# A cross-interaction network on one core: chunks 4 and 5 loaded instead of picked, and a new order of TensorE's front

## The chip, the core and the metric

The kernel runs on one NeuronCore of one Trainium2 chip. The core has TensorE (PE, with its weight loads as PEld), VectorE (DVE), ScalarE (ACT), GpSimd (POOL) and SyncE (SP, which here only issues transfers). The metric is device time in microseconds (us), the median of several executions. The profile is of one further execution.

## The reference

The input is x, 64 rows of 32 fields of 64 numbers (`X0`, float32). Three layers are computed, and of each only the sum over the embedding goes into the result:

```
Xi = X0
for W, b in ((W1, b1), (W2, b2), (W3, b3)):
    Wr = W.reshape(128, 32, m)                   # m = fields of Xi: 32, 128, 128
    Xi = einsum('bhd,bmd,ohm->bod', X0, Xi, Wr) + b[None, :, None]
    pools.append(Xi.sum(axis=-1))
y = concatenate(pools) @ fc_W.T + fc_b           # 64 x 1
```

## The kernel before

The kernel has 64 x 64 = 4096 columns (row, embedding), cut into eight **chunks** of 512. For each chunk the 128 partitions of four tiles hold products of two fields (`z`), split into a high and a low part in fp32r: `feat[:, c, 0]` (hi) and `feat[:, c, 1]` (lo). TensorE multiplies them by two sets of weights: W1's (`w1_hi`, `w1_lo`) give x1 (`x1_product(c)`, 13 matmuls), and weights `a_hi`, `a_lo` folded from W3, fc_W and W2 give the factor by which x1 is multiplied (`a_product(c)`, 14 matmuls). VectorE forms that product (`product(c)`), GpSimd adds the chunks up (`gather`), and a few small matmuls give y.

**How a chunk's features are made.** The left factor is loaded (`x_in`, four buffers). The right factor is made in one of two ways. For a chunk below `PICKED` (6 before), TensorE picks it out of the split input with 0/1 weights: `pick_right(c, half)` (L567), two matmuls for each half, into PSUM (`z_ps`). For chunks from `PICKED` on, SP loads 1 MB of ready-made factors into `r_in[:, c % 2]` (`load_right`, L185). VectorE multiplies (`mult`, L461, L477), ScalarE copies the high part (`hi`, L366, L360), and the low part is the difference: of half 0 on VectorE (`lo`, L479, L484), of half 1 on GpSimd (`lo`, L262, L266). Half 0 of the product lies in PSUM (`z_ps`), half 1 in SBUF (`r_in`). `split_x(c)` splits the input itself, on ScalarE (L362) and then GpSimd (L254, L259); a picked chunk needs it before its picks, a loaded one only for the linear matmul at the end of `a_product(c)` (L627).

**The fold of the second weights.** `v_part` (L631) contracts W3 with fc_W, a transpose and three small copies give `v_st`, four `a_round`s (L657) contract it with W2, ScalarE saves each (`save_a`), SP stores each with three transfers (`store_a`, L203 to L206), reads them back skewed into `f1` (L233 to L240), and ScalarE's queue reads `f2` (L432). VectorE adds them (L530, L532) and splits them (`main_lo`, L493, and `rest_lo`, L498).

**Order.** Every engine's program is written out by hand and runs in order; semaphores tie them together. What matters below:

- SP: after W1's rest (L222) come `load_x(5)`, `load_x(6)`, the twelve stores, the reads of `f1`, `load_right(6)`, `x16` again for `xsum`, `load_x(7)`, `load_right(7)`.
- ScalarE: hi(3,1), W1's rest (L421), split_x(5), hi(4,0), hi(4,1), save_x1(0), save_x1(1), four transfers of `f2`, hi(5,0), hi(5,1), save_zz(1).
- VectorE: chunks 0 to 5, W1's `rest_lo` after mult(4,1), then the fold's adds, chunk(6), product(0), product(1), chunk(7), product(2) and on.
- GpSimd: split_x and lo in turn; after lo(5) split_x(6), the four adds of `xsum` (L345), lo(6), split_x(7), lo(7), gathers. The features of chunk 7 lie where `xsum` is still being read (`features_free`, L148), so hi(7), lo(7) wait for it.
- TensorE: the front (L670 to L708), then x1_product(2), (3), (4), a_product(0), (1), x1_product(5), a_product(2), x1_product(6), a_product(3), x1_product(7), a_product(4) to (7). x1_product(c) for c of 2 or more waits for save_x1(c - 2), since there are two banks; a_product(c) waits for product(c - 2).

Of the kernel before, what the change touches and what calls it, by code (L numbers as in the profile page):

```python
# [24 lines left out]
TERM_HI, TERM_LO, TERM_HI2, TERMS = 0, 32, 64, 96  # L25


PICKED = 6
X_BUFS = 4


# [6 lines left out]
def cin_kernel(nc, x, xl, xr, w1, w2, w3, vecs, fc_b, out):  # L38
# [9 lines left out]
    with ctx:  # L48
# [67 lines left out]
        r_here = [sem(f"r_here{i}") for i in range(2)]  # L116
# [27 lines left out]
        def count(c, half):  # L144

            return HALVES * c + half + 1
# [30 lines left out]
        @block.sync  # L177
        def _(sp):
            def load_x(c):
                if c >= X_BUFS:  # L180
                    sp.wait_ge(z_done, count(c - X_BUFS, 1))
                    sp.wait_ge(xs_lo, c - X_BUFS + 1)
                sp.dma_start(x_in[:, c % X_BUFS, :], xl[:, c * N:(c + 1) * N]).then_inc(x_here[c % X_BUFS], 16)  # L183

            def load_right(c):  # L185
                if c % 2 == 0:
                    sp.wait_ge(spread_done, 3)
                else:
                    sp.wait_ge(hi_done, count(PICKED - 1, 1))
                    sp.wait_ge(lo_done[1], PICKED)  # L190
                sp.dma_start(r_in[:, c % 2, :, :], xr[c]).then_inc(r_here[c % 2], 16)

            def load_w3(i):
                part = slice(i * 2 * M, (i + 1) * 2 * M)
                sp.dma_start(w3_sb[:, :, :].rearrange("q (g i) o -> q g (i o)", g=4)[:, :, part],  # L195
                             w3.rearrange("q (g io) -> q g io", g=4)[:, :, part]).then_inc(w3_in[i], 16)

            def load_w2(t):
                part = slice(t * N, (t + 1) * N)
                sp.dma_start(w2_sb[:, :].rearrange("o (g n) -> o g n", g=2)[:, :, part],  # L200
                             w2.rearrange("o (g n) -> o g n", g=2)[:, :, part]).then_inc(w2_in[t], 16)

            def store_a(rows, g, t, left):  # L203

                sp.dma_start(bass.AP(scratch.tensor, (left + FIELDS * t) * M, [[EXT * M, rows], [1, FIELDS * M]]),
                             at_sb[64 * g:64 * g + rows, t, :]).then_inc(a_out, 16)  # L206

            load_x(0)
            sp.dma_start(w1_sb[:, :, 0:TILES, :], w1[:, :, 0:TILES, :]).then_inc(w1_in, 16)
            load_x(1)  # L210
            load_w3(0)
            load_w3(1)
            load_x(2)
            load_w3(2)
            load_w3(3)
            load_x(3)
            load_w2(0)
            load_w2(1)
            load_x(4)
            load_w2(2)  # L220
            load_w2(3)
            sp.dma_start(w1_sb[:, :, EVEN:, :], w1[:, :, EVEN:, :]).then_inc(w1_rest_in, 16)  # L222
            load_x(5)
            load_x(6)
            for t in range(ROUNDS):
                sp.wait_ge(a_saved, t + 1)
                store_a(EXT, 0, t, 0)
                store_a(EXT, 1, t, HALF)
                store_a(H, 0, t, H)
            sp.wait_ge(zeros_done, ZEROS)  # L230
            sp.wait_ge(a_out, A_OUT)
            for j in range(J):
                sp.dma_start(f1[H * j:H * j + H, 0:TILES, :], bass.AP(  # L233
                    scratch.tensor, EXT * TILES * j * M, [[(EXT + 1) * M, H], [EXT * M, TILES], [1, M]])).then_inc(f_main_in, 16)
            for e in range(2):
                for f, first in ((f1, HALF * EXT), (f2, HALF)):
                    sp.dma_start(f[e:TERMS:2, EVEN + e, :], bass.AP(
                        scratch.tensor, first * M, [[0, 3], [(EXT + 1) * M, HALF], [1, M]])).then_inc(f_rest_in, 16)
            sp.dma_start(f1[0:TERMS, LIN, :], bass.AP(
                scratch.tensor, FC2_COL * EXT * M, [[0, 3], [M, H], [1, M]])).then_inc(f_rest_in, 16)  # L240
            load_right(PICKED)
            sp.wait_ge(lo16_done, 1)
            sp.dma_start(x16[:, :, :].rearrange("p g n -> p (g n)"),
                         x.rearrange("h (c n) -> (h c) n", c=4)).then_inc(xp_in, 16)
            load_x(7)
            load_right(PICKED + 1)
            sp.dma_start(fcb_sb[:, :], fc_b).then_inc(fcb_in, 16)
            sp.wait_ge(y_done, 1)
            sp.dma_start(out, y_sb[:, :]).then_inc(out_done, 16)
            sp.wait_ge(out_done, 16)  # L250

        @block.gpsimd
        def _(pool):
# [22 lines left out]
            for i, base in enumerate((0, H, -H)):  # L276
# [43 lines left out]
            pool.wait_ge(xs_lo, 4)  # L320
            lo(1)
            pool.wait_ge(lo_done[1], 2)
            split_x(4)
            pool.wait_ge(xs_lo, 5)
            lo(2)
            pool.wait_ge(w1_rest_in, 16)
            nc.gpsimd.tensor_tensor(w1_sb[:, 0, EVEN:, :], w1_sb[:, 0, EVEN:, :], w1_sb[:, 1, EVEN:, :],
                                    ALU.add).then_inc(w_sum, 1)
            pool.wait_ge(w_sum, 2)
            split_x(5)  # L330
            pool.wait_ge(xs_lo, 6)
            lo(3)
            lo(4)
            lo(5)
            pool.wait_ge(lo_done[1], 6)
            split_x(6)
# [21 lines left out]
        def _(act):  # L358
# [50 lines left out]
            copy(v_st[:, H:H + 8], v_by_field[:, 0, :]).then_inc(v_saved, 1)  # L409
            copy(v_st[:, H + 8:H + 15], v_by_field[:, 1, 0:7]).then_inc(v_saved, 1)  # L410
            hi(2, 0)
            split_x(4)
            hi(2, 1)
            save_a(0)
            save_a(1)
# [3 lines left out]
            hi(3, 1)  # L419
            act.wait_ge(w_sum, 2)  # L420
            copy(w1_hi[:, EVEN:, :], w1_sb[:, 0, EVEN:, :]).then_inc(w_hi_done, 1)  # L421
            split_x(5)
            hi(4, 0)
            hi(4, 1)
            act.wait_ge(vec_in, 16)
# [4 lines left out]
            for j in range(J):  # L430
                k = 1 if j == 0 else 0
                act.dma_start(f2[H * j:H * j + H, k:TILES, :], bass.AP(  # L432
                    scratch.tensor, (TILES * j + k) * M, [[(EXT + 1) * M, H], [1, (TILES - k) * M]])).then_inc(f_main_in, 16)
            hi(5, 0)
            hi(5, 1)
            save_zz(1)
            act.wait_ge(v_saved, 1)
            copy(v_rep[:, :, :], v_st[:, 0:H].rearrange("o (h r) -> o h r", r=1).to_broadcast(
# [4 lines left out]
            save_x1(3)  # L443
            act.wait_ge(f_sum, 2)
            copy(a_hi[0:TERMS, TILES:, :], f1[0:TERMS, TILES:, :]).then_inc(a_hi_done, 1)
            split_x(6)
            save_x1(4)
            act.wait_ge(q_ready, 1)
            copy(q_sb[:, :], q_ps).then_inc(q_saved, 1)
            hi(6, 0)  # L450
            hi(6, 1)
            split_x(7)
# [7 lines left out]
        def _(dve):  # L460
            def mult(c, half):  # L461
                tiles = of_half(half)
                dve.wait_ge(x_here[c % X_BUFS], 16 * (c // X_BUFS + 1))
                if c < PICKED:
                    dve.wait_ge(picked, count(c, half))
                    right = field_bank(c, half)
                    if half == 1 and c >= 2:
                        dve.wait_ge(hi_done, count(c - 2, 1))
                        dve.wait_ge(lo_done[1], c - 1)
                else:  # L470
                    dve.wait_ge(r_here[c % 2], 16)
                    right = r_in[:, c % 2, tiles, :]
                    if half == 0:
                        dve.wait_ge(z_done, count(c - 1, 1))
                        dve.wait_ge(lo_done[0], c - 1)
# [38 lines left out]
            nc.vector.tensor_tensor(x16[:, 0, :], x16[:, 0, :], x16[:, 1, :], ALU.mult).then_inc(z16_done, 1)  # L514
            mult(0, 0)
            mult(0, 1)
            dve.wait_ge(w_hi_done, 1)
            main_lo(w1_sb[:, 0, :, :], w1_hi, w1_lo, w_lo_done)
            lo(0)
            chunk(1)  # L520
            chunk(2)
            chunk(3)
            mult(4, 0)
            mult(4, 1)
            dve.wait_ge(w_hi_done, 2)
            rest_lo(w1_sb[:, 0, :, :], w1_hi, w_lo_done)
            lo(4)
            chunk(5)
            dve.wait_ge(f_main_in, F_MAIN)
            nc.vector.tensor_tensor(f1[:, 0:TILES, :], f1[:, 0:TILES, :], f2[:, 0:TILES, :], ALU.add).then_inc(f_sum, 1)  # L530
            dve.wait_ge(f_rest_in, F_REST)
# [5 lines left out]
            dve.wait_ge(f_sum, 2)  # L537
            dve.wait_ge(a_hi_done, 2)
            rest_lo(f1, a_hi, a_lo_done)
            chunk(6)  # L540
            product(0)
            product(1)
# [18 lines left out]
        def _(pe):  # L561
# [19 lines left out]
                    nc.tensor.matmul(bank, weights[:, k, :], feat[:, c, part, k, :],  # L581
                                     start=(start and k == 0), stop=False)

            def x1_hi(c, half):
                if c >= 2 and half == 0:
                    pe.wait_ge(x1_saved, c - 1)
                pe.wait_ge(w_hi_done, 1)
                pe.wait_ge(hi_done, count(c, half))
                terms(x1_ps[c % 2][:, :], c, half, w1_hi, 0, start=(half == 0))
                pe.wait_ge(w_lo_done, 1)  # L590
                terms(x1_ps[c % 2][:, :], c, half, w1_lo, 0)

            def x1_lo(c, half):
                pe.wait_ge(lo_done[half], c + 1)
# [79 lines left out]
            pick_right(0, 1)  # L674
            keep_clock(6)
            spread16(0)
            pick_right(1, 0)
            x1_hi(0, 0)
            pick_right(1, 1)
            x1_lo(0, 0)  # L680
            v_part(0)
            v_part(1)
            v_part(2)
            pick_right(2, 0)
            v_part(3)
            pick_right(2, 1)
            pe.wait_ge(ident_done, 2)
            pe.wait_ge(vt_saved, 1)
            nc.tensor.transpose(v_ps, vt_sb[:, :], ident[:, :]).then_inc(v_ready, 1)
            x1_hi(0, 1)  # L690
            a_round(0)
            pick_right(3, 0)
            a_round(1)
            pick_right(3, 1)
            a_round(2)
            a_round(3)
            pick_right(4, 0)
            x1_lo(0, 1)
            pick_right(4, 1)
            x1_hi(1, 0)  # L700
            x1_lo(1, 0)
            x1_hi(1, 1)
            pick_right(5, 0)
            x1_lo(1, 1)
            x1_tail(0)
            x1_tail(1)
            pick_right(5, 1)
            spread16(1)  # L708
            x1_product(2)
            x1_product(3)  # L710
# [79 lines left out]
```

## Time and profile before

| | us |
|---|---|
| median of 3 runs | 82.0 (81.88 to 83.26) |
| the profiled execution, its own time | 82.64 |
| its span, first to last instruction | 80.8 |
| PE busy | 75.0 (93% of the span, 372 instructions) |
| DVE, ACT, POOL busy | 47.1, 34.6, 49.8 |
| transfers | 12.01 MB |

The span is what the engines' rows cover; the time of the execution is 1.8 us longer. A matmul of 512 columns shows 0.39 us in a group's mean, because matmuls overlap; how many start per microsecond is read from the timeline, where the next group begins before the last one's end.

### The profile page before, as it was taken

The numbers are of one execution on the slowest core, as the hardware profiler recorded it, in microseconds if no ns is written. First come the engines' busy times: TensorE is split into PE (matmuls) and PEld (weight loads), VectorE is DVE, ScalarE is ACT, GpSimd is POOL, SyncE is SP. The second block draws the span as 40 slices with busy tenths as digits, with TensorE's granted clock in tenths as the row PEclk, the third lists the DMA queues.
The fourth block names the chain that finished last, engine by engine and source line by source line (L and its number), as shares of the span: only waits on it lengthen the run. The fifth ranks groups of instructions, "written<-read, shape, count | busy, mean of one in ns | idle before, by whom it ended". The sixth has DMA issues, their size and how long they took to land.

```text
span 80.8 us, 1130 instructions
## 1 busy us (share of the span) xinstructions
PE 75.0 (93%) x372; PEld 51.7 (64%) x372; DVE 47.1 (58%) x44; ACT 34.6 (43%) x51; POOL 49.8 (62%) x49
## 2 busy tenths in 40 slices
PE   4999699989999999959999999999999999999970
PEld 1326255743218677648888888888888888886850
DVE  1056999996797998497499709973003003113541
ACT  1833994579779943983836500580300300000000
POOL 4989836999993699492099989629924103261400
PEclk9999999999999999999999999999999999999999
DMA  0998999999996434369992000000000000000000
GB/s 22 252 366 250 369 370 352 381 385 392 375 322 196 128 89 110 101 215 385 353 417 89 4 4 0 4 0 0 0 0 0 0 0 8 0 0 0 0 0 0
DMA packets 7529, 12.01 MB, mean 149 GB/s; under 512 B 835, under 2 KB 3971, under 8 KB 7267
## 3 DMA queue, kind: packets, MB, share of 16 engines
q1 hardware_dynamic: 6915, 11.16, 40.3%
q10 hardware_dynamic: 608, 0.77, 3.0%
q8 instruction: 3, 0.05, 0.3%
q14 instruction: 3, 0.02, 0.1%
HBM read 10.88 MB, written 1.05 MB: 148 GB/s over the span
## 4 chain that ended last, share of the span: by engine, by line
PE 61%; DMA 14%; SPq 13%; ACT 4%; ACTq 2%; issue 2%; DVE 1%; DVEq 0%
PE a_ps L581 28%; PE x_ps L581 21%; DMA w_sb<-w 14%; SPq L183 6%; SPq L195 3%; SPq L200 2%; ACT feat L360 2%; PE x_ps L601 2%; PE a_ps L628 2%; PE z_ps L575 2%; PE a_ps L627 2%; ACTq L432 2%; PE a_ps L666 1%; PE x_ps L739 1%; ACT zz L360 1%
## 5 line engine op out<-in xcount | busy, mean ns | idle before, releaser
L266 POOL TENSOR_TENSOR feat<-r_in,feat 128x1024 fp32r<-128x1024 f32 x8 | 19.2, 2404 | 4.1 <-ACT feat L360 3.6
L581 PE MATMUL x_ps<-feat,w_hi 128*128 128x512 f32 x64 | 18.8, 393 | 0.0
L504 DVE SCALAR_TENSOR_TENSOR x<-a_ps,vec,x 128x512 f32<-128x512 f32 x7 | 5.3, 751 | 19.2 <-PE a_ps L628 19.1
L581 PE MATMUL a_ps<-feat,a_hi 128*128 128x512 f32 x64 | 16.2, 395 | 0.0
L259 POOL TENSOR_TENSOR xs<-x_in,xs 32x512 fp32r<-32x512 f32 x7 | 10.8, 1548 | 8.1 <-ACT xs L360 7.8
L273 POOL TENSOR_TENSOR x<-x 128x512 f32<-128x512 f32 x6 | 7.8, 1292 | 11.5 <-DVE x L504 11.3
L581 PEld LDWEIGHTS x_ps<-feat,w_hi 128*128 128x128 f32 x64 | 11.9, 188 | 2.6
L581 PEld LDWEIGHTS a_ps<-feat,a_hi 128*128 128x128 f32 x64 | 11.9, 188 | 2.7
L360 ACT ACTIVATE feat<-z_ps 128x1024 fp32r<-128x1024 f32 x8 | 8.2, 1025 | 7.4 <-DVE z_ps L477 6.2
L484 DVE TENSOR_TENSOR feat<-z_ps,feat 128x1024 fp32r<-128x1024 f32 x8 | 9.7, 1218 | 2.1 <-ACT feat L360 2.1
L374 ACT ACTIVATE x<-x_ps,vec 128x512 f32<-128x512 f32 x8 | 5.4, 686 | 12.3 <-PE x_ps L601 12.3
L581 PE MATMUL x_ps<-feat,w_lo 128*128 128x512 f32 x32 | 9.9, 391 | 0.0
L360 ACT ACTIVATE feat<-r_in 128x1024 fp32r<-128x1024 f32 x8 | 8.4, 1051 | 1.7 <-DVE r_in L477 1.7
L575 PE MATMUL z_ps<-xs,pick 128*128 128x512 f32 x24 | 8.8, 457 | 0.3
L581 PE MATMUL a_ps<-feat,a_lo 128*128 128x512 f32 x32 | 8.6, 390 | 0.0
L477 DVE TENSOR_TENSOR z_ps<-x_in,z_ps 128x1024 f32<-128x1024 f32 x6 | 7.3, 1224 | 1.4 <-PE z_ps L575 1.3
L575 PEld LDWEIGHTS z_ps<-xs,pick 128*128 128x128 f32 x24 | 4.1, 204 | 5.9 <-issue 4.6
L477 DVE TENSOR_TENSOR r_in<-x_in,z_ps 128x1024 f32<-128x1024 f32 x6 | 7.3, 1215 | 0.4 <-PE z_ps L575 0.4
L565 PE MATMUL x_ps<-at_sb 128*128 128x512 bf16 x17 | 6.3, 543 | 1.2 <-DVE at_sb L507 1.2
L581 PEld LDWEIGHTS x_ps<-feat,w_lo 128*128 128x128 f32 x32 | 6.0, 188 | 1.4
L581 PEld LDWEIGHTS a_ps<-feat,a_lo 128*128 128x128 f32 x32 | 6.0, 188 | 1.3
L360 ACT ACTIVATE xs<-x_in 128x512 fp32r<-128x512 f32 x8 | 5.0, 626 | 2.2 <-DMA x_in<-xl 2.1
(76 smaller groups left out, 75.3 us busy)
## 6 DMA issues: line engine op xcount, KB each, us to landing
w_sb<-w SPq DMA_DIRECT2D x9, 512.0 KB, 8.8
x_in<-xl SPq DMA_DIRECT2D x8, 256.0 KB, 7.4
r_in<-xr SPq DMA_DIRECT2D x2, 1024.0 KB, 6.1
a_by_fields<-at_sb SPq DMA_DIRECT2D x8, 96.0 KB, 2.1
x<-x ACTq DMA_DIRECT2D x1, 512.0 KB, 4.6
x<-x SPq DMA_DIRECT2D x1, 512.0 KB, 6.0
w_sb<-w SPq DMA_DIRECT2D x1, 256.0 KB, 11.7
a_by_fields<-at_sb SPq DMA_DIRECT2D x4, 64.0 KB, 2.1
```

What stands on the lines that cost most here:

```text
L183: sp.dma_start(x_in[:, c % X_BUFS, :], xl[:, c * N:(c + 1) * N]).then_inc(x_here[c % X_BUFS], 16)
L259: nc.gpsimd.tensor_tensor(xs[rows, c, :], x_in[rows, c % X_BUFS, :], xs[rows, c, :].bitcast(f32), ALU.subtract).then_inc(xs_lo, 1)
L266: nc.gpsimd.tensor_tensor(feat[:, c, 1, of_half(1), :], z_of(c, 1), feat[:, c, 0, of_half(1), :].bitcast(f32), ALU.subtract).then_inc(lo_d ...
L273: nc.gpsimd.tensor_tensor(x1[:, 0, :], x1[:, 0, :], x1[:, c, :], ALU.add).then_inc(acc_done, 1)
L360: return nc.scalar.activation(dst, src, ACT.Copy)
L374: nc.scalar.activation(x1[:, c, :], x1_ps[c % 2][:, :], ACT.Identity, bias=vec[:, 0:1]).then_inc(x1_saved, 1)
L477: nc.vector.tensor_tensor(z_of(c, half), left, right, ALU.mult).then_inc(z_done, 1)
L484: nc.vector.tensor_tensor(feat[:, c, 1, of_half(0), :], z_of(c, 0), feat[:, c, 0, of_half(0), :].bitcast(f32), ALU.subtract).then_inc(lo_d ...
L504: nc.vector.scalar_tensor_tensor(out=x1[:, c, :], in0=a_ps[:, c % 2, :], scalar=vec[:, 3:4], in1=x1[:, c, :], op0=ALU.add, op1=ALU.mult).t ...
L565: nc.tensor.matmul(x1_ps[1][:, :], blank[:, 0:M], blank[:, 0:N], start=True, stop=True)
L575: last = nc.tensor.matmul(field_bank(c, half)[:, k, :], pick[:, half * PER_HALF + k, :], xs[:, c, :], start=True, stop=True)
L581: nc.tensor.matmul(bank, weights[:, k, :], feat[:, c, part, k, :], start=(start and k == 0), stop=False)
```

## The change

Chunks 4 and 5 are loaded too: `PICKED` is 4, SP issues a load of 1 MB for chunk 4 ahead of `load_x(5)`, one for chunk 5 where chunk 6's was, and those for 6 and 7 later. VectorE, ScalarE and GpSimd do chunk 5, and split_x(4) and (5), later. VectorE does lo(0) ahead of W1's low part. On TensorE the picks of chunks 4 and 5 are gone, x1's product of chunk 0 is cut in two functions and spread ahead of the picks and of `v_part`, and the rounds of the fold stand in pairs.

```diff
-PICKED = 6
+PICKED = 4
@@ sync, load_right
-                if c % 2 == 0:
+                if c == PICKED:
                     sp.wait_ge(spread_done, 3)
                 else:
-                    sp.wait_ge(hi_done, count(PICKED - 1, 1))
-                    sp.wait_ge(lo_done[1], PICKED)
+                    sp.wait_ge(hi_done, count(max(c - 2, PICKED - 1), 1))
+                    sp.wait_ge(lo_done[1], max(c - 1, PICKED))
@@ sync, program
             sp.dma_start(w1_sb[:, :, EVEN:, :], w1[:, :, EVEN:, :]).then_inc(w1_rest_in, 16)
+            load_right(4)
             load_x(5)
             load_x(6)
...
-            load_right(PICKED)
+            load_right(5)
             sp.wait_ge(lo16_done, 1)
...
             load_x(7)
-            load_right(PICKED + 1)
+            load_right(6)
+            load_right(7)
@@ gpsimd
-            split_x(4)
-            pool.wait_ge(xs_lo, 5)
             lo(2)
             (W1's rest is added)
+            lo(3)
+            lo(4)
+            pool.wait_ge(lo_done[1], 5)
+            split_x(4)
             split_x(5)
             pool.wait_ge(xs_lo, 6)
-            lo(3)
-            lo(4)
             lo(5)
@@ scalar
             hi(2, 0)
-            split_x(4)
             hi(2, 1)
...
             copy(w1_hi[:, EVEN:, :], w1_sb[:, 0, EVEN:, :]).then_inc(w_hi_done, 1)
-            split_x(5)
             hi(4, 0)
             hi(4, 1)
...
-            hi(5, 0)
-            hi(5, 1)
             save_zz(1)
...
-            split_x(6)
             save_x1(4)
             act.wait_ge(q_ready, 1)
             copy(q_sb[:, :], q_ps).then_inc(q_saved, 1)
+            split_x(4)
+            hi(5, 0)
+            hi(5, 1)
+            split_x(5)
+            split_x(6)
             hi(6, 0)
@@ vector
+            lo(0)
             dve.wait_ge(w_hi_done, 1)
             main_lo(w1_sb[:, 0, :, :], w1_hi, w1_lo, w_lo_done)
-            lo(0)
             chunk(1)
             chunk(2)
             chunk(3)
-            mult(4, 0)
-            mult(4, 1)
             dve.wait_ge(w_hi_done, 2)
             rest_lo(w1_sb[:, 0, :, :], w1_hi, w_lo_done)
-            lo(4)
-            chunk(5)
+            chunk(4)
             dve.wait_ge(f_main_in, F_MAIN)
...
             rest_lo(f1, a_hi, a_lo_done)
+            chunk(5)
             chunk(6)
@@ tensor: x1_hi is cut into x1_main (w1_hi) and x1_low_weights (w1_lo)
+            x1_main(0, 0)
             pick_right(1, 0)
-            x1_hi(0, 0)
             pick_right(1, 1)
+            x1_main(0, 1)
             x1_lo(0, 0)
+            x1_low_weights(0, 0)
+            x1_low_weights(0, 1)
             v_part(0)
             v_part(1)
             v_part(2)
             pick_right(2, 0)
+            pick_right(2, 1)
             v_part(3)
-            pick_right(2, 1)
             (transpose of vt)
-            x1_hi(0, 1)
+            x1_lo(0, 1)
+            pick_right(3, 0)
             a_round(0)
-            pick_right(3, 0)
             a_round(1)
+            x1_hi(1, 0)
             pick_right(3, 1)
             a_round(2)
             a_round(3)
-            pick_right(4, 0)
-            x1_lo(0, 1)
-            pick_right(4, 1)
-            x1_hi(1, 0)
             x1_lo(1, 0)
             x1_hi(1, 1)
-            pick_right(5, 0)
             x1_lo(1, 1)
             x1_tail(0)
             x1_tail(1)
-            pick_right(5, 1)
             spread16(1)
```

`mult`'s wait for `r_here` counts the loads of its buffer.

## Rows read from the trace of the kernel before

**Rows 1.** The chain that ended last: start, duration, and what ran.
```profile
11.53 11.71 DMA w_sb<-w
23.29 1.08 PE a_ps L666 x4
...
34.29 0.91 ACT zz L360
...
38.73 2.74 PE x_ps L581 x12
...
48.38 2.77 PE x_ps L581 x12
```

**Rows 2.** Timeline of TensorE: start, duration, operation, count, idle time before.
```profile
24.30 0.74 PE L575 MATMUL z_ps<-xs,pick 128*128 128x512 f32 x2
...
31.39 0.62 PE L581 MATMUL x_ps<-feat,w_hi 128*128 128x512 f32 x2
...
35.24 0.50 PE L601 MATMUL x_ps<-zz,w_hi 96*128 96x512 f32 x1 [0.97 <-ACT zz L360]
```

**Rows 3.** Timeline of ScalarE between 24 and 32 us.
```profile
24.41 0.60 ACT L360 ACTIVATE at_sb<-a_ps 128x512 f32<-128x512 f32 x1 [0.56 <-PE a_ps L666]
24.91 1.05 ACT L360 ACTIVATE feat<-r_in 128x1024 fp32r<-128x1024 f32 x1
25.86 0.41 ACT L360 ACTIVATE w_hi<-w_sb 128x256 fp32r<-128x256 f32 x1
...
29.82 0.69 ACT L374 ACTIVATE x<-x_ps,vec 128x512 f32<-128x512 f32 x1 [1.18 <-PE x_ps L601]
```

**Rows 4.** Timeline of VectorE, the same columns.
```profile
27.52 0.99 DVE L498 TENSOR_TENSOR w_hi<-w_sb,w_hi 32x256 fp32r<-32x256 f32 x1
...
39.97 0.55 DVE L498 TENSOR_TENSOR a_hi<-f,a_hi 32x384 fp32r<-32x384 f32 x1 [1.15 <-ACT a_hi L360]
40.55 1.23 DVE L477 TENSOR_TENSOR z_ps<-x_in,r_in 128x1024 f32<-128x1024 f32 x1
41.81 2.19 DVE L477 TENSOR_TENSOR r_in<-x_in,r_in 128x1024 f32<-128x1024 f32 x1
43.92 1.21 DVE L484 TENSOR_TENSOR feat<-z_ps,feat 128x1024 fp32r<-128x1024 f32 x1
45.26 0.75 DVE L504 SCALAR_TENSOR_TENSOR x<-a_ps,vec,x 128x512 f32<-128x512 f32 x1
```

**Rows 5.** Timeline of GpSimd, the same columns.
```profile
26.95 1.28 POOL L259 TENSOR_TENSOR xs<-x_in,xs 32x512 fp32r<-32x512 f32 x1 [2.06 <-ACT xs L360]
...
34.43 2.38 POOL L266 TENSOR_TENSOR feat<-r_in,feat 128x1024 fp32r<-128x1024 f32 x1 [1.28 <-ACT feat L360]
40.55 2.36 POOL L259 TENSOR_TENSOR xs<-x_in,xs 32x512 fp32r<-32x512 f32 x1 [3.75 <-ACT xs L360]
43.05 3.48 POOL L345 TENSOR_TENSOR x<-x 128x512 f32<-128x512 f32 x3
...
47.13 2.40 POOL L266 TENSOR_TENSOR feat<-r_in,feat 128x1024 fp32r<-128x1024 f32 x1 [0.21 <-issue]
```

**Rows 6.** SP's queue: issue of transfers, start, duration and count.
```profile
21.15 5.54 SPq L205 DMA_DIRECT2D a_by_fields<-at_sb  x12
28.06 1.74 SPq L233 DMA_DIRECT2D f<-a_by_fields  x4
...
33.72 0.45 SPq L191 DMA_DIRECT2D r_in<-xr  x1
```

**Rows 7.** Transfers of r_in, then of W1's rest: from issue to landing.
```profile
DMA to landing us min/median/max: 5.0/6.1/7.1
...
DMA to landing us min/median/max: 11.7/11.7/11.7
```

**Rows 8.** Stretches: width, busy us of PE, PEld, DVE, ACT, POOL, granted clock, DMA share, GB/s.
```profile
18.00:20.00 2.00, 2.00 (x9) 0.78 (x8) 1.26 (x2) 2.00 (x6) 1.99 (x1) 1.00 1.05 386
24.00:26.00 2.00, 2.00 (x9) 1.42 (x8) 1.50 (x2) 1.59 (x3) 0.89 (x2) 1.00 0.72 208
```

More of the change, by code:

```diff
@@ L470, in mult @@
                 else:
-                    dve.wait_ge(r_here[c % 2], 16)
+                    dve.wait_ge(r_here[c % 2], 16 * ((c - PICKED) // 2 + 1))
                     right = r_in[:, c % 2, tiles, :]
@@ L582, in terms, with x1_main @@
                                      start=(start and k == 0), stop=False)
-            def x1_hi(c, half):
+            def x1_main(c, half):
                 if c >= 2 and half == 0:
@@ L589, in x1_hi, with x1_low_weights @@
                 terms(x1_ps[c % 2][:, :], c, half, w1_hi, 0, start=(half == 0))
+            def x1_low_weights(c, half):
+                pe.wait_ge(hi_done, count(c, half))
                 pe.wait_ge(w_lo_done, 1)
                 terms(x1_ps[c % 2][:, :], c, half, w1_lo, 0)
+            def x1_hi(c, half):
+                x1_main(c, half)
+                x1_low_weights(c, half)
             def x1_lo(c, half):
```

## The prediction

> **What bounds the kernel now.** I read the chain of waits first. From 23.29 us on it is TensorE almost alone: x1 and a products at 13 or 14 matmuls each, 12 matmuls in 2.74 to 2.77 us, so 0.23 us a matmul [rows 1]. The one hole is 0.97 us ahead of x1's tail of chunk 2, which waits for ScalarE's copy of zz, and that copy ends at 35.2 behind hi(5,0) and hi(5,1) [rows 1, 2]. Ahead of 23.29 the chain is W2's last quarter, 11.71 us from issue to landing [rows 1], on a queue that moves 386 GB/s with its engines full [rows 8]. So an edit gains in two ways only: by fewer matmuls or holes behind 23.29, and it loses wherever TensorE must wait for features. The timelines of ScalarE, VectorE and GpSimd say how near those waits are.
>
> **TensorE's own work.** The change removes the picks of chunks 4 and 5: four halves of two matmuls, 8 x 0.23 = 1.8 us. Behind the last round of the fold (starts 23.29, ends 24.4 [rows 1]; chunk 4's load is issued after W2 and W1's rest, so this stays) TensorE now has only x1_lo(1,0), x1_hi(1,1), x1_lo(1,1), 8 matmuls, to 26.2. Before, it had work without a hole from 24.30 to 31.39 and beyond [rows 2]. The reordered front ahead of 23.29 gains nothing that lasts, since the landing of W2 ends it: its moved matmuls lie there beside VectorE's multiplies. It costs nothing either, by the same cover. Pick_right(3,1) comes some 0.5 us later, mult(3,1) ends near 23.8, and hi(3,1) was held by save_a(3) until 24.91 anyway [rows 3].
>
> **The low part of W1's rest.** The tails of chunks 0 and 1 need it. ScalarE's order gives hi(3,1) at 24.91 to 25.96 and W1's rest at 25.86 to 26.27, as before [rows 3]. GpSimd's lo(3) needs only hi(3,1), so it starts at 26.0 and runs 2.40 us, as another lo does [rows 5], to 28.4. VectorE asks for rest_lo (L498) at 26.3. Rows 4 and 5 show what happens then: this line took 0.99 us from 27.52 while GpSimd's subtraction ran from 26.95 to 28.23, 0.55 us at 39.97 with GpSimd idle. It ended 0.28 us after GpSimd's ended. So rest_lo ends at 28.4 + 0.3 = 28.7. Before, this work was hidden behind picks; now TensorE waits from 26.2 to 28.7. The bound below is 26.9 (no block).
>
> **Chunk 4.** Its load of 1 MB lands behind W1's rest, which was issued at 12.3 and landed 11.7 us later, at 24.0 [rows 7]. At 386 GB/s [rows 8] 1.05 MB is 2.7 us: 26.7, so it is not what chunk 4 waits for. VectorE's in-order queue is. mult(4,0) runs 28.7 to 29.9 and mult(4,1) to 31.0 (1.23 us [rows 4], 1.1 for the second), with GpSimd idle. hi(4,1) ends at 32.1, and save_x1(0), queued behind it on ScalarE, takes 0.69 us [rows 3] to 32.8. x1_product(2) waits for that save. Before it began at 31.39 [rows 2]; between the tails with spread16(1) (to 30.1) and 32.8 TensorE waits another 2.7 us. The product's 12 matmuls end at 35.55. ScalarE's zz no longer waits behind hi(5): it issues f2 near 31.1 to 33.3 and has zz at 34.4, so the hole of 0.97 us is gone. The tail starts at 35.5 against 35.24 before. Sum up to here: **+0.25 us**. The 1.8 us of picks and the 0.97 us hole are all spent on the two new waits. x1_product(4) ends at 41.95 for 41.7 [rows 1].
>
> **The transfers behind.** Twelve stores of the fold, issued from 21.15, flowed at once; the last landed by 28.0, when the reads of f1 start [rows 6]. Now 2.7 us of load stands ahead of them in the same queue. The stores have slack in rate (208 GB/s at share 0.72 [rows 8]), so I put the last landing 1.4 us later, between 0.8 and 2.7. The loads issued from 33.72 [rows 6] shift with it: chunk 5's lands at 38.8 + 1.4 = 40.2 (5.0 us from issue [rows 7]), chunk 6's where chunk 7's was, near 44.0 + 1.4 = 45.4, bounds 44.8 and 46.7. The f1 and f2 sums have room: a_hi is needed only at 41.95, nearly 10 us after f2's transfers are issued.
>
> **Chunks 5 to 7.** Here GpSimd gets a chain that it did not have. ScalarE's queue after save_x1(4) (ends 42.7) is: q, split_x(4) to 43.3, hi(5,0), hi(5,1) to 45.15, split_x(5) to 45.7. Only then GpSimd does split_x(5), lo(5), split_x(6), xsum, lo(6). Before, lo(5) was over at 36.8 [rows 5] and this chain began at 40.55 with split_x(6). Alone these take 1.28 + 2.40 + 1.28 + 2.9 + 2.40 us with 0.5 between: 56.5 for lo(6). And VectorE's multiplies of loaded chunks block them. Rows 4 and 5: mult(6,0) and split_x(6) started together at 40.55; the multiply took 1.23, the split 2.36 instead of 1.28 us. mult(6,1) from 41.81 took 2.19 and ended 1.1 us after the split, and the adds, started at 43.05, took 3.48. So each such multiply puts 1.1 us into GpSimd's chain, and waits out the operation in flight.
>
> The Trainium skill (SBUF — State Buffer, "Who interferes with whom") speaks against the change in the same way: a VectorE instruction with two SBUF inputs contends with a GpSimd instruction that reads SBUF, whole instruction against whole instruction, and one with a PSUM input does not. By it moving two chunks' right factors from PSUM to SBUF makes four more such multiplies; the rows above agree at 1.1 us each. Were it a shared bandwidth instead, the sum would be about 1 us less.
>
> With chunk 6's load at 45.4: mult(6,0) 45.45 to 46.6, split_x(5) to 47.9, mult(6,1) to 49.0, lo(5) to 51.4. x1_product(5) starts at 48.6 (6.7 us after 41.95 [rows 1]) and wants lo(5) after 10 matmuls, at 50.9: wait 0.5. lo(6): 51.4 + 1.3 + 3.0 + 2.6 = 58.3; x1_product(6) starts 6.2 us after 49.1, at 55.3, and wants it at 57.6: wait 0.75. Then mult(7,0) to 59.5, split_x(7) to 60.8, mult(7,1) to 61.9, hi(7,1) to 63.0, lo(7) to 65.4; x1_product(7) wants it at 64.55: wait 0.9. Together 2.15 us. With the load at 46.7, mult(6,0) loses its turn to split_x(5): mult(6,1) ends at 51.65, lo(6) of VectorE and product(0), queued behind it, at 53.6, and a_product(2) waits 2.0 us for product(0) (before, product(0) was over at 46.0 [rows 4]); one more wait of 0.4. Both orders give about the same.
>
> **Sum.** 0.25 + 2.2 to 2.5 = 2.5 us. Span 80.8 to 83.3; the profiled execution was 82.64, 0.6 us above the median of 82.0, so against the median 84.5.
>
> **Rivals.**
> (1) The chain after 41.95 is milder: no block by multiplies, loads on time. Then lo(6) is ready at 56.5 and wanted at 57.3, nothing waits, and 0.25 us or, with rest_lo unblocked too, -1.4 us remain: 80.6 to 83.6, no change that can be told. For it: TensorE's slack at chunk 5 is 1.2 us. Against: 2.36 and 2.19 us in rows 4 and 5.
> (2) Faster. The features keep ahead all along: TensorE gives back 1.8 us of picks and 0.97 us of hole: 82.0 - 2.8 = 79.2. It decides if W1's low rest is ready by 26.2 and save_x1(0) by 27.6. For it: chunk 4's load is there by 26.7. Against: W1's high rest ends at 26.27 [rows 3] and four operations follow in series.
> (3) Slower yet. Chunk 6's load lands behind 47.1, in lo(5)'s time, and mult(6,0) waits until 49.5, product(0) until 55: a_product(2) waits 3.5 us: 82.0 + 4 = 86. Or TensorE's two waits of 2.6 us, 1.4 us of work between them, cost it the granted clock, which rows 8 show at 1.00 (2.4 GHz) throughout; then x1_product(2) and (3) at 1.2 GHz cost up to 3 us. The one hole shown, 0.97 us [rows 2], did not cost it, so this is bounded from one side only.
>
> **Chances.** My forecast 0.60 (83.7 to 85.3); rival 1 0.19; rival 2 0.06; rival 3 0.15 (85.3 to 87.5). I leave out rival 2 and the lower part of rival 1: range 82.6 to 86.6. About 2% can be told from no change here: faster 0.07, within 0.18 (rival 1, nearly whole), slower 0.75.
>
> **What the new profile would show.** W1's rest_lo (L498, first instance) at over 2 us beside a GpSimd lo of 2.4; TensorE idle near 26 to 28.7 at x1's tail and to 32.8 at x1_product(2), released by ScalarE's save; the tail of chunk 2 within 0.5 us of 35.24; stores landing over 0.8 us later; GpSimd busy without a hole from 45.7 to 58; TensorE waiting 0.5 to 2 us in or before a_product(2), again in x1_product(6). I am wrong if those multiplies do not lengthen GpSimd's operations, or if stores and loads are as early as before.

## The result and the profile after

| | median us | against the kernel before |
|---|---|---|
| the kernel before | 81.94 (81.85 to 83.26) | |
| the changed kernel | 87.93 (87.78 to 88.45) | 1.073, 95% interval 1.068 to 1.078 |

A ratio leaves disturbed executions out, so it can differ a little from the quotient of two medians.

The change makes the kernel 7.3% slower: 6.0 us, where 2.5 were forecast and 86.6 us was the upper end. The profiled execution's span grew from 80.8 to 86.2 us, by 5.4. That is less than 6.0 because the profiled execution of the kernel before took 82.64 us, 0.7 us above its median here, and that of the changed kernel 88.05 us, 0.1 us above. The direction and the first two waits were right; the size was not.

The page of the changed kernel, the slices of the granted clock:

```profile
PEclk9999999999999965579999999999999999999999
```

The line before showed nines throughout; here four slices between 30 and 39 us are low. Its stretches by hand (width, busy us of PE, PEld, DVE, ACT, POOL, granted clock, DMA share, GB/s):

```profile
26.80:29.30 2.50, 0.10 (x1) 0.00 (x0) 2.47 (x2) 0.00 (x0) 2.14 (x1) 1.00 0.60 203
29.30:31.00 1.70, 1.63 (x6) 0.96 (x6) 1.67 (x2) 0.42 (x1) 0.00 (x0) 0.92 0.07 22
31.00:33.40 2.40, 0.17 (x1) 0.00 (x0) 1.96 (x2) 2.23 (x4) 0.42 (x1) 0.50 0.42 117
33.40:38.40 5.00, 4.94 (x13) 3.93 (x14) 0.69 (x1) 1.80 (x4) 1.94 (x1) 0.59 0.51 153
38.40:44.50 6.10, 6.10 (x29) 5.01 (x29) 2.78 (x4) 2.31 (x4) 0.00 (x0) 1.00 0.98 377
```

TensorE stands still twice, for 2.5 and 2.4 us, with 1.6 us of work between. Its clock falls from 2.4 to 1.2 GHz: first in the stretch behind the first hole (0.92), and it is down all through the second. Windows of 0.5 us put the fall near 30.7 us and the return near 37.5 us. x1_product(2), 13 matmuls, takes from 33.4 to 38.4 us; at full clock it takes 3 (the next one, 38.44 to 41.40).

Timeline of TensorE, the changed kernel (start, duration, operation, count, idle time before and its releaser):

```profile
29.37 0.71 PE L610 MATMUL x_ps<-zz,w_hi 96*128 96x512 f32 x2 [2.46 <-DVE w_hi L501]
...
33.46 1.22 PE L582 MATMUL x_ps<-feat,w_hi 128*128 128x512 f32 x2 [2.30 <-ACT x L377]
...
53.82 0.73 PE L582 MATMUL x_ps<-feat,w_hi 128*128 128x512 f32 x2 [0.30 <-POOL feat L269]
...
60.96 0.74 PE L582 MATMUL x_ps<-feat,w_hi 128*128 128x512 f32 x2 [0.60 <-POOL feat L269]
```

The first two rows are the two holes, each with the releaser that was forecast: W1's low rest on VectorE, and ScalarE's save_x1(0). They answer to the unbroken stretch of [rows 2]. VectorE in the same kernel:

```profile
26.80 2.42 DVE L501 TENSOR_TENSOR w_hi<-w_sb,w_hi 32x256 fp32r<-32x256 f32 x1 [1.35 <-ACT w_hi L363]
29.25 1.23 DVE L480 TENSOR_TENSOR z_ps<-x_in,r_in 128x1024 f32<-128x1024 f32 x1
...
58.82 3.18 DVE L480 TENSOR_TENSOR z_ps<-x_in,r_in 128x1024 f32<-128x1024 f32 x1 [4.87 <-issue]
61.91 2.31 DVE L480 TENSOR_TENSOR r_in<-x_in,r_in 128x1024 f32<-128x1024 f32 x1
```

L501 took 0.99 us before [rows 4] and 2.42 here, beside GpSimd's lo(3), the first row of GpSimd below. mult(7,0) starts at 58.8 only. ScalarE, late in the kernel:

```profile
64.25 1.06 ACT L363 ACTIVATE feat<-r_in 128x1024 fp32r<-128x1024 f32 x1 [1.11 <-DVE r_in L480]
65.22 1.25 ACT L377 ACTIVATE x<-x_ps,vec 128x512 f32<-128x512 f32 x2
```

The save in the second row is save_x1(5), ready long before, queued behind hi(7,1). x1_product(7) needs its bank and starts at 65.94. GpSimd:

```profile
26.60 2.34 POOL L269 TENSOR_TENSOR feat<-r_in,feat 128x1024 fp32r<-128x1024 f32 x1 [3.10 <-ACT feat L363]
...
50.49 3.28 POOL L269 TENSOR_TENSOR feat<-r_in,feat 128x1024 fp32r<-128x1024 f32 x1
```

And SP's queue:

```profile
37.02 17.15 SPq L192 DMA_DIRECT2D r_in<-xr  x2
```

lo(5) ends at 53.8, 17 us later than before [rows 5]; the load of chunk 7 shares a buffer with chunk 5, waits for it and goes out at 53.8 too (SP's row is two issues, the second at its end), 17 us later than before.

**Where 5.4 us come from**, by the starts of TensorE's products in the timelines:

| start of | before | after | added since the row above |
|---|---|---|---|
| x1_product(2) | 31.39 | 33.46 | +2.07 |
| x1_product(3) | 35.58 | 38.44 | +0.79 (x1_product(2) at half clock +2.0, the hole for zz gone -1.2, counted by starts) |
| a_product(0) | 41.69 | 44.52 | -0.03 |
| x1_product(6) | 54.42 | 57.89 | +0.64 (lo(5)) |
| x1_product(7) | 60.63 | 65.94 | +1.84 (lo(6) 0.9, save_x1(5) 0.95) |
| a_product(4) | 63.63 | 69.03 | +0.09 |

### The profile page after: what moved, and what is told of

Same layout as the page of the kernel before. It is cut to its first block, busy times and chain, and to the rows that moved or that the text cites. A ratio compares the mean times of both kernels' runs of the same rounds, so it can differ in the third digit from the quotient of the medians.

```text
span 86.2 us, 1130 instructions
## 1 busy us (share of the span) xinstructions
PE 74.6 (87%) x364; PEld 51.7 (60%) x364; DVE 47.1 (55%) x44; ACT 34.9 (40%) x51; POOL 49.4 (57%) x49
## 3 DMA queue, kind: packets, MB, share of 16 engines
q1 hardware_dynamic: 7203, 13.26, 43.4%
## 4 chain that ended last, share of the span: by engine, by line
PE 49%; issue 15%; DVE 9%; POOL 9%; ACT 8%; DMA 7%; ACTq 1%; SPq 0%; POOLq 0%; DVEq 0%
PE x_ps L582 19%; PE a_ps L582 13%; DMA w_sb<-w 7%; DVE r_in L480 6%; PE a_ps L675 4%; PE z_ps L576 4%; ACT feat L363 4%; POOL feat L269 3%; POOL xs L262 2%; PE a_ps L648 2%; ACT x L377 2%; DVE z_ps L480 2%; POOL w_sb L308 1%; POOL z_lo L312 1%; PE x_ps L746 1%
## 5 line engine op out<-in xcount | busy, mean ns | idle before, releaser
L269 POOL TENSOR_TENSOR feat<-r_in,feat 128x1024 fp32r<-128x1024 f32 x8 | 19.9, 2491 | 10.0 <-ACT feat L363 9.5
L582 PE MATMUL x_ps<-feat,w_hi 128*128 128x512 f32 x64 | 20.7, 427 | 4.0 <-ACT x L377 3.1
L582 PE MATMUL x_ps<-feat,w_lo 128*128 128x512 f32 x32 | 10.4, 414 | 0.0
L480 DVE TENSOR_TENSOR z_ps<-x_in,r_in 128x1024 f32<-128x1024 f32 x4 | 6.9, 1718 | 4.9 <-issue 4.9
L582 PEld LDWEIGHTS x_ps<-feat,w_lo 128*128 128x128 f32 x32 | 6.6, 205 | 1.6
L480 DVE TENSOR_TENSOR r_in<-x_in,r_in 128x1024 f32<-128x1024 f32 x4 | 7.1, 1771 | 0.1
L480 DVE TENSOR_TENSOR z_ps<-x_in,z_ps 128x1024 f32<-128x1024 f32 x4 | 4.9, 1226 | 1.4 <-PE z_ps L576 1.4
L480 DVE TENSOR_TENSOR r_in<-x_in,z_ps 128x1024 f32<-128x1024 f32 x4 | 4.9, 1217 | 1.3 <-issue 1.3
```

The costliest lines, as they stand in the source:

```text
L269: nc.gpsimd.tensor_tensor(feat[:, c, 1, of_half(1), :], z_of(c, 1), feat[:, c, 0, of_half(1), :].bitcast(f32), ALU.subtract).then_inc(lo_d ...
L480: nc.vector.tensor_tensor(z_of(c, half), left, right, ALU.mult).then_inc(z_done, 1)
```

## The experiments

The theory after this reading: the loads of chunks 4 and 5 are early enough, and the loss comes from orders behind them, in two places, plus the clock. The rivals: one place hides the other (what the front gives back is waited for later); the new front of TensorE costs it; the loads themselves are too late.

**The clock: fill the holes.** `e1_fill`, on the changed kernel:

```diff
             x1_lo(1, 1)
+            pe.wait_ge(a_saved, ROUNDS)
+            fill(a_ps[:, 0, :], 10)          # ten matmuls whose result is overwritten
             x1_tail(0)
             x1_tail(1)
             spread16(1)
+            pe.wait_ge(lo_done[0], 4)
+            fill(z_ps[:, 1, 0, :], 9)
```

> The changed kernel with 10 idle-time matmuls (into a bank of a_ps that is free) between x1_lo(1,1) and x1's first tail, and 9 (into a free bank of z_ps) after spread16(1): they fill the two holes of 2.5 and 2.3 us and compute nothing. Theory (clock): the granted clock, at half from 30.7 to 37.5 us in the changed kernel, stays at 1.00, x1_product(2)'s twelve matmuls take 2.8 instead of 4.9 us, and all behind follows: 87.9 - 2.1 = 85.8 us. Rival (the chain of chunks 5 to 7 on GpSimd, VectorE and the loads sets the end): what the front gives back is waited for again at x1_product(5) to (7): 87.3 or more.

Measured: 86.18 us, 1.053 (1.046 to 1.060) of before. Stretches of this kernel:

```profile
26.80:29.30 2.50, 2.38 (x11) 1.62 (x9) 2.47 (x2) 0.00 (x0) 2.19 (x1) 1.00 0.56 193
...
33.40:36.50 3.10, 2.99 (x13) 2.50 (x14) 0.00 (x0) 1.85 (x4) 2.01 (x1) 1.00 0.45 116
```

x1_product(2) starts at 33.51, as in the changed kernel, and is over 3.1 us later instead of 5 (36.59 and 38.44 us). The kernel is 1.75 us faster by doing 19 matmuls more. So the clock is a cost of its own of 1.8 to 1.9 us, and nearly none of it is taken back later.

**Which part costs: the front alone, the loads alone.** `e2_front_only` is the kernel before with only this:

```diff
@@ vector
+            lo(0)                            # ahead of W1's low part, as in the change
@@ tensor
+            x1_main(0, 0)
             pick_right(1, 0)
-            x1_hi(0, 0)
...                                           # as in the change, to a_round(3)
             pick_right(4, 0)                 # chunks 4 and 5 are still picked
-            x1_lo(0, 1)
+            x1_lo(1, 0)
             pick_right(4, 1)
-            x1_hi(1, 0)
-            x1_lo(1, 0)
             x1_hi(1, 1)
             pick_right(5, 0)
```

> The kernel before with only the new order of TensorE's front and VectorE's lo(0) ahead of W1's low part; chunks 4 and 5 are still picked, between the fold's last round and spread16(1). Theory (the front is bounded by the landing of W2 and hides its order): 82.0 us, within 0.5 us of the kernel before. Rival (the order itself delays save_a(3) and hi(3,1), 0.5 us later in the changed kernel, and with them all of chunk 4): 82.5 to 83 us. Rival (it is the good half of the change): 81 or less.

Measured: 82.89 us, 1.009 (1.006 to 1.013). That is small but clear of no change, and it is the first rival's time: ScalarE's save_a(3) starts at 25.10 us instead of 24.41, and what stands behind it on ScalarE comes 0.7 us later. The timeline of TensorE has a hole that the kernel before lacks, for the split that chunk 5's picks need; the x1 matmuls that covered it have been moved ahead:

```profile
28.95 0.72 PE L575 MATMUL z_ps<-xs,pick 128*128 128x512 f32 x2 [1.38 <-POOL xs L259]
```

The changed kernel has no such picks, so this hole can't occur there. The run shows that the new front by itself is no gain and delays ScalarE; the 0.9% is not its price in the changed kernel.

`e4_loads_only` is the other half: the changed kernel with TensorE's front, and VectorE's lo(0), in the order of the kernel before.

> The changed kernel with TensorE's front and VectorE's start in the order of the kernel before, less the picks of chunks 4 and 5: only the part of the change that loads chunks 4 and 5. Theory (the loads and what follows from them are the whole loss, and the new front only makes the first hole longer, since its matmuls have been moved ahead of it): W1's low rest still late at 28.7, so x1_product(2) near 33; the first hole is 1.2 instead of 2.5 us. If the clock holds, 85.3 us; if it still falls, 87.4. Rival (the new front is what costs): near 83.

Measured: 88.14 us, the median of five executions between 86.86 and 89.02; 1.059 (1.054 to 1.063). So the loads and what was reordered for them are most of the loss, 5.9% of 7.3%, not the whole of it; the rest comes only with the new front, which makes the first hole 1.3 us longer. The two holes are still there:

```profile
29.92 0.71 PE L610 MATMUL x_ps<-zz,w_hi 96*128 96x512 f32 x2 [1.14 <-DVE w_hi L501]
34.02 1.22 PE L582 MATMUL x_ps<-feat,w_hi 128*128 128x512 f32 x2 [2.46 <-ACT x L377]
```

The first is shorter, as expected, and the clock fell all the same, here inside the second hole: it read 1.00 up to 32.0 us and 0.50 from 32.5 us. This trace is of the longest execution, 89.02 us, and its clock fell once more, in the front (0.51 from 11.5 to 15.0 us), behind holes of 1.48 and 0.46 us:

```profile
PEclk9999965999999985559999999999999999999998
```

**The lock on rest_lo.** `e7_w1rest_first`, on the changed kernel:

```diff
-            hi(3, 1)
             act.wait_ge(w_sum, 2)
             copy(w1_hi[:, EVEN:, :], w1_sb[:, 0, EVEN:, :]).then_inc(w_hi_done, 1)
+            hi(3, 1)
```

> The changed kernel with one swap on ScalarE: the high part of W1's rest is copied ahead of hi(3,1). Then VectorE's rest_lo can start before GpSimd's lo(3) does. Theory (rest_lo took 2.4 us because a GpSimd instruction that reads SBUF was in flight): L501's first instance takes 0.55 us and ends near 26.4 instead of 29.2, x1's tails run at 26.5 to 27. The start of x1_product(2) moves little, since mult(4,1) now meets lo(3): near 32.8. The two holes become one of 4.5 us, so the clock falls for certain: 87 to 88.5 us. Rival (rest_lo is slow by itself on this data): it still takes over 2 us.

Measured: 87.08 us, 1.057 (1.050 to 1.063). VectorE:

```profile
25.94 0.42 DVE L501 TENSOR_TENSOR w_hi<-w_sb,w_hi 32x256 fp32r<-32x256 f32 x1 [0.40 <-ACT w_hi L363]
...
27.86 3.26 DVE L480 TENSOR_TENSOR r_in<-x_in,r_in 128x1024 f32<-128x1024 f32 x1
```

The same instruction on the same data takes 0.42 instead of 2.42 us once GpSimd is idle. Now mult(4,1) pays, 3.26 us, since lo(3) got its turn between VectorE's two multiplies. x1_product(2) starts at 32.83 after one hole of 4.44 us, and the clock falls again (0.59 from 32.8 to 37.0), not in the hole but 0.7 us behind its end.

**The save behind chunk 4's copies.** `e3_save_first`, on the changed kernel:

```diff
-            hi(4, 0)
-            hi(4, 1)
             act.wait_ge(vec_in, 16)
             save_x1(0)
             save_x1(1)
+            hi(4, 0)
+            hi(4, 1)
```

> The changed kernel with ScalarE's save_x1(0) and save_x1(1) ahead of hi(4,0) and hi(4,1). Theory (x1_product(2) waits for a save that is queued behind chunk 4's copies): x1_product(2) starts near 31.1 instead of 33.46, the second hole is gone, the clock stays at 1.00 or falls only briefly, the tail of chunk 2 waits for zz to about 35.2 instead of 38.2; 87.9 - 3.1 = 84.8 us, with 1.3 us of new hole ahead of that tail. Rival (the later chain of chunks 5 to 7 takes it back): 87 or more. Rival (the clock falls all the same because of the first hole): 86 to 87.

Measured: 87.03 us, 1.055 (1.047 to 1.063), with executions from 85.86 to 88.50. The front gained what was expected: a_product(0) starts at 41.32 instead of 44.52, and the hole of 1.3 us forecast ahead of x1's tail of chunk 2 did not come. But of these 3.2 us the median keeps 0.9, which the theory had not foreseen and its first rival had. The trace is of the longest execution, 88.50 us, and shows what can take it back; how much of it the shorter ones had is not shown:

```profile
54.46 3.78 PE L582 MATMUL a_ps<-feat,a_hi 128*128 128x512 f32 x8 [3.46 <-DVE x L507]
```

VectorE, ahead of it:

```profile
47.29 3.11 DVE L480 TENSOR_TENSOR z_ps<-x_in,r_in 128x1024 f32<-128x1024 f32 x1 [2.26 <-DMA r_in<-xr]
50.32 2.29 DVE L480 TENSOR_TENSOR r_in<-x_in,r_in 128x1024 f32<-128x1024 f32 x1
```

Chunk 6's load landed at 47.3, inside lo(5)'s time on GpSimd; both multiplies were blocked in turn, and product(0), behind them on VectorE, held a_product(2) for 3.46 us. That is the prediction's rival 3, its first case, to the letter, though in this kernel and not in the changed one. The clock fell here too, twice (at the end of the hole in the front, and inside this one of 3.46 us), and the first fall is of use. Stretches around the front's hole:

```profile
26.80:29.20 2.40, 0.00 (x0) 0.00 (x0) 2.37 (x2) 0.00 (x0) 2.01 (x1) 0.99 0.54 196
29.20:32.00 2.80, 2.77 (x7) 2.01 (x8) 2.37 (x2) 1.91 (x3) 0.00 (x0) 0.50 0.18 51
```

The first hole alone, 2.46 us, was enough for it. Without the second hole it came back near 32.6 us, before x1_product(2) was far on: that product took 3.3 us, not 5.

**GpSimd's order.** `e5_lo5_first`, on e1_fill:

```diff
-            split_x(4)
-            split_x(5)
-            pool.wait_ge(xs_lo, 6)
             lo(5)
-            split_x(6)
             (xsum)
             lo(6)
-            split_x(7)
+            split_x(4)
+            split_x(5)
             lo(7)
+            split_x(6)
+            split_x(7)
```

> The kernel of e1_fill (holes of the front filled, clock held, 86.2 us) with GpSimd's lo(5), the adds of xsum and lo(6) ahead of split_x(4), (5) and (6); these splits come around lo(7), where their only reader, the linear matmul of a_product(4) on, has time. Theory (GpSimd's chain, made longer by VectorE's blocked multiplies, is what x1_product(5) to (7) wait for, 2.6 us in all): lo(5) ends near 49 instead of 53.8, chunk 7's load is issued 4 us sooner; the waits in x1_product(5), (6) and (7) go, but a_product(2) now waits about 1.3 us for product(0), which stands behind chunk 6 on VectorE: 84.9 us. Rival (the loads' landing sets them): 86 us, no gain.

Measured: 85.25 us, 1.034 (1.027 to 1.042). The waits of x1_product(5) to (7) are gone; one is left, of the size expected:

```profile
53.73 2.11 PE L586 MATMUL a_ps<-feat,a_hi 128*128 128x512 f32 x8 [1.24 <-DVE x L507]
```

`e6_product0_early`, on e5_lo5_first:

```diff
             chunk(5)
-            chunk(6)
+            mult(6, 0)
             product(0)
+            mult(6, 1)
+            lo(6)
             product(1)
@@ scalar
+            save_x1(5)
             hi(7, 0)
             hi(7, 1)
-            save_x1(5)
```

> The kernel of e5_lo5_first, with VectorE's product(0) right behind mult(6,0) instead of behind chunk 6, and ScalarE's save_x1(5) ahead of hi(7,0). Theory (with the order on GpSimd, VectorE and ScalarE mended, all that is left of the loss is the late start of x1_product(2), 33.5 against 31.4, less the hole of 1 us that is gone): 83.4 us. Rival (something else in chunks 5 to 7, as the loads): 84.9 us or more.

Measured: 83.65 us, 1.015 (1.009 to 1.021). Behind a_product(0) TensorE now takes exactly what it took before (42.63 to 64.57 for the start of a_product(4); before 41.69 to 63.63). So the loss behind a_product(0), 2.6 us, is one of order on three engines and not of the loads: VectorE did wait 1.19 us for chunk 6's load, to 47.42, but no hole of TensorE came of it.

**All orders mended.** `e8_reordered` is the changed kernel without fillers, with e7's, e3's, e5's and e6's edits, and:

```diff
             save_x1(0)
             save_x1(1)
+            save_zz(1)                       # was behind f2's transfers
@@ vector: main_lo(f1, a_hi, a_lo, a_lo_done) ahead of the wait for f_rest_in
```

> The changed kernel, no fillers, with all the orders mended at once: W1's rest ahead of hi(3,1), save_x1(0), (1) and save_zz(1) ahead of hi(4,0) and of f2's transfers, GpSimd's and VectorE's order as in e6_product0_early, save_x1(5) ahead of hi(7,0), and VectorE's main_lo of the second weights ahead of the wait for f's rest. Theory (loading chunks 4 and 5 is sound, and the orders behind it lose the time): x1_product(2) starts near 28, product(4) ends near 38 instead of 41.5 in the kernel before, and then it depends on the loads of chunks 5 to 7: 79 to 80.5 us, faster than before. Rival (the loads, 2.7 us more of them ahead of the fold's stores, or the f weights, are late in themselves): TensorE waits at a_product(0) or x1_product(5), the clock falls, 82 us or more.

Measured: 83.19 us (80.85 to 84.51), not told apart from before. It has both outcomes in it: 80.85 in the execution where the clock stayed up, 82.9 to 84.5 where it fell. In the profile:

```profile
50.02 3.43 PE L584 MATMUL a_ps<-feat,a_hi 128*128 128x512 f32 x8 [2.14 <-DVE x L507]
```

and on VectorE

```profile
47.54 1.77 DVE L480 TENSOR_TENSOR z_ps<-x_in,r_in 128x1024 f32<-128x1024 f32 x1 [3.10 <-DMA r_in<-xr]
```

TensorE is now so far ahead that chunk 6's load is waited for. The forecast of 79 to 80.5 us did not hold; the rival, that a load is late in itself, did, and the next run shows that the queue's order made it late. `e9_load6_sooner`, on e8_reordered:

```diff
             load_right(5)
+            load_right(6)
             (x16 again)
             load_x(7)
-            load_right(6)
@@ vector
             chunk(5)
-            mult(6, 0)
             product(0)
+            mult(6, 0)
             mult(6, 1)
```

> The kernel of e8_reordered with chunk 6's load issued right behind chunk 5's, ahead of x16 and load_x(7), and VectorE's product(0) ahead of mult(6,0). In e8_reordered mult(6,0) waited for that load until 47.5, and a_product(2) 2.1 us for product(0) behind it; the clock fell there in three of four executions. Theory (these two orders are what is left): the load lands near 45, a_product(2) waits at most 0.5 us, the clock holds: 79.5 to 80.8 us, faster than the kernel before. Rival (the loads as such come too late for a TensorE that is 4 us ahead): x1_product(5) or (6) waits 2 us or more for its features, the clock falls again in some executions: 82 us or more.

Measured: 80.93 us, 0.984 (0.977 to 0.992) of the kernel before, granted clock 1.00 in all four executions. That is 1.6% faster than before, and 0.1 us above the forecast's upper end. a_product(2) no longer waits. It is the fastest that keeps the loads; a_product(0) starts at 37.16, 4.5 us ahead of the kernel before, and 3.2 of these are lost again by a_product(4) to three waits for lo(5), lo(6) and lo(7) on GpSimd and one for the second weights:

```profile
40.45 0.47 PE L638 MATMUL a_ps<-xs,a_hi 96*128 96x512 f32 x1 [0.30 <-DVE a_hi L501]
...
47.38 0.74 PE L584 MATMUL x_ps<-feat,w_hi 128*128 128x512 f32 x2 [0.70 <-POOL feat L269]
...
54.57 0.74 PE L584 MATMUL x_ps<-feat,w_hi 128*128 128x512 f32 x2 [0.72 <-POOL feat L269]
...
61.54 0.73 PE L584 MATMUL x_ps<-feat,w_hi 128*128 128x512 f32 x2 [0.48 <-POOL feat L269]
```

As a measure of what the loads are worth, `e10_before_zz` moves one line in the kernel before:

```diff
             save_x1(1)
+            save_zz(1)
...
             hi(5, 0)
             hi(5, 1)
-            save_zz(1)
```

> The kernel before with one move on ScalarE: save_zz(1) right behind save_x1(1), ahead of f2's transfers and hi(5). Theory (in the kernel before TensorE has one hole behind 24 us, 0.97 us for zz, and nothing else near it): x1_product(3) follows without a hole, 1 us less, 81.0 us. Rival (f2's transfers or hi(5), 1 us later, are waited for instead): 82 us.

Measured: 81.21 us, 0.989 (0.982 to 0.995). The hole of 0.97 us is gone and nothing takes its place. The intervals of e9 and e10 overlap, and e9 holds this move as well: the loads, with all the edits around them, bring no more than can be told from one moved line.

## Why the prediction was right or wrong

- **The step that failed: the clock, a term that the sum puts at nothing.** The sum prices TensorE's two waits at their length and x1_product(2) at 0.23 us a matmul, as if the granted clock stayed at 1.00. It fell to 1.2 GHz and x1_product(2) took 5.0 us instead of 3. With the holes filled the clock stayed up and the kernel was 1.75 us faster (e1). This is 1.9 of the 3.4 us between the forecast of 84.5 and the measured 87.9. It stood in rival 3, which has a share of 0.15, and was argued away by a hole of 0.97 us that had not cost it. That row said nothing of a hole of 2.5 us, and no other row did. The mechanism was named and its chance was too low: the two holes were my own forecast, so their consequence should have been in the main case. Its price was misread too: 3 us is what one product of 13 matmuls loses at half clock, so x1_product(2) and (3) together would have lost 6; the first one lost 2, the second nothing.
- **Picks removed, 1.8 us; hole for zz gone, 1 us; both spent in the front.** Right. With the orders mended (e9) TensorE is 3.3 us ahead at x1_product(2) and 4.5 us at a_product(0), so the gain was there.
- **"It costs nothing either, by the same cover"** (the front's new order). Wrong, by 0.5 us. I let save_a(3) stay at 24.41 us [rows 3]; it came at 24.91, since x1_hi(1,0) now stands ahead of the last two rounds, which begin at 22.93 and no longer wait for W2. hi(3,1), rest_lo and chunk 4 all moved with it. "Gains nothing that lasts" seems wrong as well: six x1 matmuls (1.4 us) now stand ahead of the last round, and the 3.3 us of e9 are more than the picks. No run takes this gain apart.
- **rest_lo blocked by lo(3).** Right in place, size and cause: forecast to end at 28.7, it ended at 29.2, 0.5 of it from the step above; e7 shows the cause.
- **x1_product(2) behind save_x1(0), at 32.8.** The wait was right; it ended at 33.46, 0.66 us later: 0.5 from save_a(3), and the second of chunk 4's multiplies took 1.23 us instead of 1.1. e3 shows the cause. "The tail starts at 35.5 against 35.24, +0.25 us" was the sum's worst term: the tail started at 38.21, and a_product(0) +2.83 us late. Of that miss, 1.9 us is the clock and 0.66 the later start.
- **The transfers 1.4 us late.** The reads of f1 begin at 29.9 instead of 28.1, 1.8 us late; chunk 5's load is issued at 35.6, where chunk 6's was at 33.7. Wrong for chunk 6's load: forecast to land at 45.4, at worst 46.7, it landed between 46.9 and 47.5 wherever VectorE waited for it (e3, e5, e6, e8). It did not matter in the changed kernel, since VectorE came to chunk 5 at 43.4 and to chunk 6 at 48.0, later still. e6 shows that the loads held nothing of TensorE behind a_product(0) at that pace.
- **GpSimd's chain and the blocked multiplies, 2.2 us.** Near in size, 2.57 measured. That GpSimd's chain holds x1_product(5) and (6) is shown by e5; what the multiplies add to it is read from rows only (lo(5) 3.28 us instead of 2.40, split_x(5) 2.04 instead of 1.28). Wrong in its last link, and the size agrees there by luck: I had x1_product(7) wait for lo(7) 0.9 us; it waited 0.95 for save_x1(5), queued behind hi(7,1), which stood there in the kernel before and was free then.
- **The rest of the miss.** Between the traces the forecast of +2.5 us misses by 2.9, between the medians by 3.4: the trace of the kernel before was of an execution above its median. That part is no term of the change.

The 5.4 us between the two traces are accounted for: 1.9 are the clock, taken back by e1; 2.57 the waits behind a_product(0), taken back by e5 and e6; the 0.94 that e6 still has at a_product(0) are the two waits of the front less the picks and the hole for zz, and e8 and e9 remove the waits.

## What to carry to other kernels

When a predicted change opens holes in TensorE's work, price the clock in the same breath: two holes of 2.5 and 2.3 us cost 1.9 us on top of themselves here, and useless matmuls in the holes bought 1.75 us back. A save, a product or a copy that frees a buffer belongs ahead of the next chunk's work in an in-order queue, and must be looked up again whenever that chunk becomes later. Moving an operand from PSUM to SBUF turns a VectorE instruction into one that takes turns with GpSimd; count the turns on GpSimd's chain as well as on VectorE's.

## What the runs showed of the hardware

- TensorE's clock went to 1.2 GHz behind a single hole of 2.46 us (e3, and the changed kernel), with holes of 1.14 and 2.46 us (e4), and behind one of 4.44 us (e7). It stayed at 1.00 in the traces with one of 0.97 us (before), with three of 0.70, 0.72 and 0.48 us that lie 7 us apart (e9), and with the holes filled (e1). With 2.14 us, and 0.63 shortly before, it fell in three of four executions (e8). A hole of two microseconds is not always needed: in the trace of e4 it also fell in the front, behind holes of 1.48 and 0.46 us. Three single executions of the kernel before, run beside the experiments, had a mean clock of 0.979 instead of 1.00 (82.92, 82.98 and 82.95 us); where it fell in them was not traced. It fell inside the hole (e8, and e4's second), at its end (e3), 0.7 us behind it (e7) or 1.3 us behind it (the changed kernel). The second hole of the changed kernel probably kept it down for x1_product(2): it was low from 30.7 to 37.5 us there, and from 29.2 to 32.6 in e3, which has no second hole. What it takes exactly these runs do not settle.
- VectorE and GpSimd take turns instruction by instruction when both of VectorE's inputs are in SBUF. One subtraction of 32 x 256 took 0.42 us (GpSimd idle, e7), 0.99 [rows 4] and 2.42 us (the changed kernel), the last two ending 0.28 us after GpSimd's instruction had ended; a multiply took 1.23 alone and up to 3.33 (e7). With one input in PSUM the same multiply took 1.22 us in the midst of two GpSimd subtractions. In the kernel before, on VectorE and on GpSimd:

```profile
30.91 1.22 DVE L477 TENSOR_TENSOR r_in<-x_in,z_ps 128x1024 f32<-128x1024 f32 x1
...
28.31 4.84 POOL L266 TENSOR_TENSOR feat<-r_in,feat 128x1024 fp32r<-128x1024 f32 x2
```

The Trainium skill (SBUF — State Buffer, "Who interferes with whom") says that whoever starts first holds the shared ports for its whole instruction; the rows agree (e7: lo(3) ended at 30.03, mult(4,1), begun at 27.86, at 31.12), and show besides that the waiting engine comes in between two instructions that its rival has back to back.
